# Order of projections, state products and token transfers in a fused attention and expert kernel

## The reference

```python
xn = layernorm(x)
x = x + attention(xn) + experts(xn)
# attention: 16 heads of 16 features, chunks of 64 tokens, sequences of 256
q = (q @ fq1_w.T + fq1_b) * (q @ fq2_w.T + fq2_b)      # k likewise with fk1, fk2
kv = cumsum over chunks of (kc^T vc), shifted by one chunk
o = (qc @ kv) + tril(qc @ kc^T) @ vc                   # state product + values
o = rms_norm_per_head(o) * norm_w; return o @ wo.T
# experts: 8, hidden 512; per token the most probable experts up to a sum of 0.9
probs = softmax(xn @ router_w.T); w = top_p_weights(probs, 0.9)
out += w[:, e] * ((silu(xn @ gate_w[e].T) * (xn @ up_w[e].T)) @ down_w[e].T)
```

## Time and profile before

| What | Value |
|---|---|
| median of 3 runs | 766.76 us (766.34 to 768.1) |
| profiled execution | 765.0 us |
| its span, first to last instruction | 763.3 us |
| mean granted TensorE clock | 0.973 |
| PE busy | 715.8 us (94%) |
| DVE busy | 495.6 us (65%) |
| ACT busy | 404.0 us (53%) |
| POOL busy | 346.1 us (45%) |

### The profile page before, as it was taken

How to read it: one execution, slowest core, us unless ns; L and a number is a source line. 1 busy time by engine, 2 the same in 40 slices (tenths; PEclk the granted TensorE clock), 3 DMA queues, 4 the chain that set the end, 5 groups by cost and what they waited for, 6 DMA issues and landing times.

```text
span 763.3 us, 19612 instructions
## 1 busy us (share of the span) xinstructions
PE 715.8 (94%) x6616; PEld 659.2 (86%) x6617; DVE 495.6 (65%) x1149; ACT 404.0 (53%) x923; POOL 346.1 (45%) x371
## 2 busy tenths in 40 slices
PE   8589999999999994799999999999999999999993
PEld 7467777777777773799999999999999999999992
DVE  5377887879788788365655754755754756656652
ACT  4236465555646546254655654655654655555551
POOL 3001202211120612266666766666766666666663
PEclk9799999999999998799999999999999999999997
DMA  2431211213120302543543643633643634543332
GB/s 93 131 85 48 66 56 55 59 52 111 34 77 28 76 9 70 178 101 58 110 97 58 136 70 56 145 63 57 134 72 57 144 63 79 120 63 57 63 60 31
DMA packets 51860, 59.58 MB, mean 78 GB/s; under 512 B 9344, under 2 KB 48256, under 8 KB 51840
## 3 DMA queue, kind: packets, MB, share of 16 engines
q0 software_dynamic: 19776, 27.16, 22.3%
q1 hardware_dynamic: 32064, 32.16, 14.2%
HBM read 37.15 MB, written 22.15 MB: 78 GB/s over the span
## 4 chain that ended last, share of the span: by engine, by line
PE 79%; DVE 11%; issue 4%; DMA 2%; ACT 2%; SPq 1%; POOL 0%; DVEq 0%; ACTq 0%; POOLq 0%
PE ring L1120 10%; PE ring L1121 10%; PE ring L1122 10%; PE A L1120 9%; PE A L1121 9%; PE A L1122 9%; DVE s_sb L801 4%; PE ring L1166 3%; PE S L1122 3%; PE S L1121 3%; PE S L1120 3%; PE A L1347 3%; PE ring L1188 3%; PE S L1194 2%; DMA xa<-x 1%
## 5 line engine op out<-in xcount | busy, mean ns | idle before, releaser
L473 POOL DMA_INDIRECT out<-ybuf,s_idx x98 | 161.8, 1651 | 62.6 <-POOL s_idx L469 46.6
L457 POOL DMA_INDIRECT xg<-gather_table,g_idx x100 | 100.5, 1005 | 88.2 <-issue 62.2
L1095 DVE TENSOR_TENSOR h_lo<-h,h_hi 128x256 fp32r<-128x256 f32 x196 | 83.5, 426 | 79.4 <-ACT h_hi L724 79.4
L724 ACT ACTIVATE h_hi<-h 128x256 fp32r<-128x256 f32 x196 | 82.0, 418 | 64.8 <-DVE h L1091 56.8
L1120 PE MATMUL ring<-w_hi,h_hi 128*128 128x256 f32 x392 | 113.7, 290 | 0.4 <-DVE h_lo L1095 0.4
L1120 PE MATMUL A<-gT_hi,w_hi 128*128 128x256 f32 x392 | 110.2, 281 | 1.8 <-DVE gT_lo L1064 1.8
L1121 PE MATMUL A<-gT_lo,w_hi 128*128 128x256 f32 x392 | 109.9, 280 | 0.0
L1122 PE MATMUL A<-gT_hi,w_lo 128*128 128x256 f32 x392 | 109.7, 280 | 0.0
L1122 PE MATMUL ring<-w_hi,h_lo 128*128 128x256 f32 x392 | 109.5, 279 | 0.0
L1121 PE MATMUL ring<-w_lo,h_hi 128*128 128x256 f32 x392 | 109.5, 279 | 0.0
L373 POOL TENSOR_TENSOR on_lo<-on,on_hi 128x512 fp32r<-128x512 f32 x15 | 19.3, 1288 | 143.4 <-ACT on_hi L534 143.4
(11 more groups left out here) (221 smaller groups left out, 2055.1 us busy)
## 6 DMA issues: line engine op xcount, KB each, us to landing
w_raw<-wffn SPq DMA_DIRECT2D x72, 192.0 KB
xa<-x SPq DMA_DIRECT2D x8, 512.0 KB, 4.7
gather_table<-xna SPq DMA_DIRECT2D x8, 512.0 KB, 3.1
xr<-x SPq DMA_DIRECT2D x8, 512.0 KB, 4.2
out<-yout SPq DMA_DIRECT2D x8, 512.0 KB
out<-ybuf,s_idx POOLq DMA_INDIRECT x104, 3.9
xg<-gather_table,g_idx POOLq DMA_INDIRECT x100
w_raw<-wqk_nat SPq DMA_DIRECT2D x1, 512.0 KB, 4.9
```

The lines of the kernel that those rows point to most:

```text
L457: pool.indirect_dma_start(out=xg[:, sub, :], out_offset=None, in_=table, in_offset=bass.IndirectOffsetOnAxis(ap=g_idx[:, sub:sub + 1], axi ...
L473: pool.indirect_dma_start(out=out, out_offset=bass.IndirectOffsetOnAxis(ap=s_idx[:, sub:sub + 1], axis=0), in_=ybuf[:, sub, :], in_offset= ...
L724: a.activation(h_hi[:, ic, :], h[:, ic, :], ACT.Copy).then_inc(hhi_ok, 1)
L1095: v.tensor_tensor(h_lo[:, ic, :], h[:, ic, :], h_hi[:, ic, :].bitcast(F32), ALU.subtract).then_inc(hlo_ok, 1)
```

## The change

Five things are reordered; no instruction is added or taken away.

1. SP sends the first normalised tokens to the table and loads the second 512 tokens before it waits for the split and loads the first expert's weights.
2. At the end of a round and in the set-up, the first half's queries are projected and multiplied before its keys, with the banks exchanged (queries in A3 and A0, keys in A1 and A2). ACT masks these queries at the end of the round before instead of at its start, ahead of t2k and of the second half's `head_rstd`; DVE makes queries and keys before the second half's `head_norm`. PE makes the first scores before value product 1.
3. In `values`, the two state products (now `earlier_chunk`) come before quarter 0 of a half and open its sum; the values are added to them.
4. DVE makes the first half of the one-hot before it masks the first state, in rounds 1 to 6.
5. In round 0 DVE takes the third step of the choice after masked scores 4 and 5.

```diff
--- before.py
+++ after.py
@@ -228,8 +228,8 @@
                        (S_both[:, :, :], ring[:, 1:3, :]), (S_both[:, :, :], ring[:, 1:3, :])]
         ring_first = (1, 1, 0, 1)
 
-        k_banks = [(A[3], A[0]), (A[0], A[3])]
-        q_banks = [(A[1], A[2]), (A[1], A[2])]
+        k_banks = [(A[1], A[2]), (A[0], A[3])]
+        q_banks = [(A[3], A[0]), (A[1], A[2])]
         values_banks = [A[0], A[1], A[3], A[3]]
         kt_banks = [A[0], A[1]]
         wo_banks = [A[3], A[0]]
@@ -239,7 +239,7 @@
         ms_banks = S
         xt_banks = [A[3], A[0]]
 
-        fused_order = [(3, A[0]), (2, A[3]), (1, A[2]), (0, A[1])]
+        fused_order = [(1, A[0]), (0, A[3]), (3, A[2]), (2, A[1])]
 
         names = ("small_in vo_in natural masks counts feat_ok fused_ps fused_ok split_ok setup_dve setup_act "
                  "x_in xn_ok xt_ps xhi_ok xlo_ok lg_ok proj_ps t2_ok qk_ok qz_ok xstat_ok v_ps v_ok kt_ps kt_ok kv_ps kv_ok "
@@ -277,17 +277,17 @@
             sp.dma_start(wvr_raw, wvr).then_inc(vo_in, DMA)
             sp.dma_start(wo_raw, wo).then_inc(vo_in, DMA)
 
+            def tokens_out(s):
+                sp.dma_start(table_blk[s][:, :, 0:D], xna[:, :, :]).then_inc(table_in, DMA)
+
+            sp.wait_ge(xn_ok, 1)
+            tokens_out(0)
+            sp.dma_start(xa[:, :, :], x_blk[1]).then_inc(x_in, DMA)
             sp.wait_ge(split_ok, 2)
             for piece in range(PIECES):
                 cols = slice(piece * PW, (piece + 1) * PW)
                 sp.dma_start(w_raw[:, cols], wffn[0][:, cols]).then_inc(w_in, DMA)
 
-            def tokens_out(s):
-                sp.dma_start(table_blk[s][:, :, 0:D], xna[:, :, :]).then_inc(table_in, DMA)
-
-            sp.wait_ge(xn_ok, 1)
-            tokens_out(0)
-            sp.dma_start(xa[:, :, :], x_blk[1]).then_inc(x_in, DMA)
 
             def round_of(s, first, last, more):
                 if not first:
@@ -550,7 +550,7 @@
 
             def keys2(s, half):
 
-                act.wait_ge(proj_ps, 8 * s + (1, 7)[half])
+                act.wait_ge(proj_ps, 8 * s + (3, 7)[half])
                 a.activation(t2k[:, half, :], k_banks[half][1][:, :], ACT.Identity,
                              bias=smalls[:, 4 * DK + 3:4 * DK + 4]).then_inc(t2_ok, 1)
 
@@ -567,14 +567,14 @@
 
             def queries_masked(s, half):
 
-                act.wait_ge(qk_ok, 4 * s + half + 2)
+                act.wait_ge(qk_ok, 4 * s + (1, 3)[half])
                 for par in range(2):
                     last = a.activation(qz[:, half, par, :], q[:, half, :], ACT.Copy, scale=parity[:, par:par + 1])
                 last.then_inc(qz_ok, 1)
 
             def queries2(s, half):
 
-                act.wait_ge(proj_ps, 8 * s + (3, 5)[half])
+                act.wait_ge(proj_ps, 8 * s + (1, 5)[half])
                 a.activation(t2q[:, half, :], q_banks[half][1][:, :], ACT.Identity, bias=bq2[:, 0:1],
                              scale=DK ** -0.5).then_inc(t2_ok, 1)
 
@@ -606,7 +606,6 @@
 
             def round_of(s, first, last):
 
-                queries_masked(s, 0)
                 values_out(s, 0)
                 values_out(s, 2)
                 values_out(s, 1)
@@ -639,10 +638,11 @@
                     return
                 squares(s, 1)
                 head_rstd(s, 0)
+                queries2(s + 1, 0)
+                heads_hi(s, 0)
+                queries_masked(s + 1, 0)
                 keys2(s + 1, 0)
-                heads_hi(s, 0)
                 head_rstd(s, 1)
-                queries2(s + 1, 0)
 
             token_rstd(0)
             norm_apply(0, True)
@@ -660,8 +660,9 @@
             fused_hi(3)
             act.wait_ge(setup_dve, 1)
             act.wait_ge(counts, 1)
+            queries2(0, 0)
             keys2(0, 0)
-            queries2(0, 0)
+            queries_masked(0, 0)
             round_of(0, True, False)
             with act.Fori(1, NBLK - 1) as s:
                 round_of(s, False, False)
@@ -781,15 +782,15 @@
 
             def queries(s, half):
 
-                dve.wait_ge(t2_ok, 4 * s + half + 2)
-                dve.wait_ge(proj_ps, 8 * s + (4, 6)[half])
+                dve.wait_ge(t2_ok, 4 * s + (1, 3)[half])
+                dve.wait_ge(proj_ps, 8 * s + (2, 6)[half])
                 v.scalar_tensor_tensor(q[:, half, :], q_banks[half][0][:, :], smalls[:, 4 * DK:4 * DK + 1], t2q[:, half, :],
                                        ALU.add, ALU.mult).then_inc(qk_ok, 1)
 
             def keys(s, half):
 
-                dve.wait_ge(t2_ok, 4 * s + (1, 4)[half])
-                dve.wait_ge(proj_ps, 8 * s + (2, 8)[half])
+                dve.wait_ge(t2_ok, 4 * s + (2, 4)[half])
+                dve.wait_ge(proj_ps, 8 * s + (4, 8)[half])
                 v.scalar_tensor_tensor(k[:, half, :], k_banks[half][0][:, :], smalls[:, 4 * DK + 2:4 * DK + 3],
                                        t2k[:, half, :], ALU.add, ALU.mult).then_inc(qk_ok, 1)
 
@@ -928,6 +929,8 @@
                 if not last:
                     norm_refine(s + 1, chain)
                 softmax_head(s, chain)
+                if not first and not last:
+                    one_hot(s - 1, 0)
                 state(s, 0)
                 queries(s, 1)
                 if last:
@@ -940,7 +943,8 @@
                 choose(s, 1, chain)
                 if last:
                     add_indices(s - 1)
-                choose(s, 2, chain, first)
+                if not first:
+                    choose(s, 2, chain, first)
                 if last:
                     masked_scores(s, 4)
                     slots(s, 0, chain, last_rank_bank)
@@ -952,10 +956,10 @@
                     state(s, 1)
                     masked_scores(s, 7)
                     return
-                if not first:
-                    one_hot(s - 1, 0)
                 masked_scores(s, 4)
                 masked_scores(s, 5)
+                if first:
+                    choose(s, 2, chain, first)
                 if not first:
                     one_hot(s - 1, 1)
                 masked_scores(s, 6)
@@ -968,9 +972,9 @@
                 slots(s, 0, chain)
                 slots(s, 1, chain)
                 head_norm(s, 0, chain)
+                queries(s + 1, 0)
                 keys(s + 1, 0)
                 head_norm(s, 1, chain)
-                queries(s + 1, 0)
 
             chain = Chain(dve, dve_step, None)
             norm_stats(0, chain)
@@ -1015,8 +1019,8 @@
             v.memset(keep[:, :, :], 0.0).then_inc(yr_ok, 2)
             v.memset(sm[:, :], 0.0).then_inc(idx_ok, 1)
             dve.wait_ge(counts, 1)
+            queries(0, 0)
             keys(0, 0)
-            queries(0, 0)
             round_of(0, True, False, chain)
             dve.reg_mov(chain_reg, chain.n)
             with dve.Fori(1, NBLK - 1) as s:
@@ -1168,25 +1172,30 @@
                         if n == 1:
                             last.then_inc(s_ps, 1)
 
+            def earlier_chunk(s, half):
+
+                pe.wait_ge(kv_ok, 2 * s + half + 1)
+                for b in range(2):
+                    second = slice((2 * b + 1) * P, (2 * b + 2) * P)
+                    mm(O[half][:, second], kv[:, half, b, :], q[:, half, second], start=(b == 0), stop=True,
+                       skip_group_check=True)
+
             def values(s, quad):
 
                 half, chunk = quad // 2, quad % 2
                 if quad == 0:
                     pe.wait_ge(v_ok, TT * s + TT)
-                if chunk == 1:
-
-                    pe.wait_ge(kv_ok, 2 * s + half + 1)
-                    for b in range(2):
-                        second = slice((2 * b + 1) * P, (2 * b + 2) * P)
-                        mm(O[half][:, second], kv[:, half, b, :], q[:, half, second], start=False, stop=True,
-                           skip_group_check=True)
-                pe.wait_ge(s_ok, NPAIR * s + 2 * (quad + 1) + (1 if chunk == 0 else 0))
+                if chunk == 0:
+                    pe.wait_ge(s_ok, NPAIR * s + 2 * quad + 3)
+                    earlier_chunk(s, half)
+                else:
+                    pe.wait_ge(s_ok, NPAIR * s + 2 * quad + 2)
                 for n in range(4):
                     t, par = n // 2 * 2 + chunk, n % 2
                     for g in range(PAIRS):
                         w = vz[:, t, half * PAIRS + g, 2 * par:2 * par + 2, :].rearrange("p a d -> p (a d)")
                         last = mm(O[half][32 * g:32 * g + 32, t * P:(t + 1) * P], w, s_sb[:, (PAIRS * quad + g) % NS, n, :],
-                                  start=(chunk == 0 and n == 0), stop=True, skip_group_check=True, tile_position=(0, 32 * g))
+                                  start=False, stop=True, skip_group_check=True, tile_position=(0, 32 * g))
                 last.then_inc(pv_ps, 1)
 
             def mean_squares(s, half):
@@ -1215,7 +1224,7 @@
                 o.then_inc(wo_ps, 1)
 
             def keys_by_token(s, half):
-                pe.wait_ge(qk_ok, 4 * s + (1, 4)[half])
```

(19 more changed lines are left out.)

## The result

The changed kernel takes **756.4 us** (median of 4 runs, 754.72 to 756.92), the kernel before 766.82 beside it (766.34 to 768.1): a ratio of 0.9854 [0.984, 0.9868], so 10.4 us less. The forecast was 5.3 us less: its sign and its largest term held, its size did not. The profiled execution spans 755.2 us and took 756.91.

What follows compares the result with a forecast made beforehand. PE was taken to bound a round, with DVE close behind. The sum -10.1 + 0.6 + 0.3 + 3.9 = -5.3 us took the 766.76 us median to 761.5 us; range 756.0 to 764.5, the forecast's own 758.5 to 764.5.

Steps and rivals of the forecast that it cites:

- Part 1: Set-up: second tokens loaded ahead of expert weights, first state product earlier; -10.1 us, bounds -8.2 and -10.5.
- Part 2: Round 0: choice of experts after two masked scores, PE's 2.13 us wait stays; 0 us, bounds -3.8 and +0.1.
- Part 3: State products first: PE waits for the masked state in the second half; +0.57 us in each of rounds 0 to 6.
- Part 4: Round's turn, queries before keys: late second head norm delays statistics and logits; +0.55 us per turn, bounds -0.37 and +0.8.
- Part 5: Half a one-hot moved into DVE's wait for the state product: PE's 0.34 us wait goes; -0.34 us.
- +0.78: Forecast change of a steady round, 0.55 - 0.34 + 0.57 us, paid by rounds 2 to 6.
- The first: Rival: rounds gain as edits suggest, PE's 0.71 us idleness goes in six rounds; -14.4 us, 752.4 us; chance 0.12.
- The second: Rival: new waits drop PE's clock behind the fourth value product, seven turns, 11.9 us in all; 773.4 us; chance 0.06.
- The third: Rival: set-up, second tokens still land near 28.8 us, so -10.1 falls away; 771.6 us; chance 0.04.

Runs made afterwards that it cites:

- part 1 alone: Kernel before with only the second tokens' load moved ahead of the expert weights on SP: 755.93 us, ratio 0.9841.
- the one with the shape alone changed: Changed kernel with state products back between the values, each 128*128 state product cut into four 128*32 ones: 753.26 us, ratio 0.9805.
- the last two kernels: Second head norm ahead of keys, state products at each half's end, one-hots and round 0 transposes moved; state products 128*32: 747.02 us, or 128*128: 746.48 us.
- state between: Changed kernel with the two state products of a half put back between its two quarters of values: 755.68 us, ratio 0.9838.
- head norm first: Changed kernel with the second head norm back ahead of the keys on ACT and DVE, queries still first: 751.78 us, ratio 0.979.
- part 4 undone: Changed kernel with keys projected before queries again at the turn of a round, banks as before: 757.25 us, ratio 0.9846.
- the last kernel of the experiments: The reordered version without PE's waits, its state products in 128*128 tiles instead of 128*32, still at each half's end: 746.48 us, ratio 0.9719.

## Why the prediction was half right

**Part 1** was right: -10.44 us at the first state product for a forecast of -10.1, no wait of PE from 14 to 35 us, clock 1.00; the kernel with part 1 alone carries the whole gain.

**Part 2** was right: PE waits 2.17 us at 37.16 instead of 2.13; nothing is won.

**Part 3 is the step that failed**, at the sentence "the four matmuls are the same, only the order differs", by which the first half of the round cost 0 and the second the whole wait. The wait itself was sized well (0.61 us for 0.57). But in their new place the state products follow a projection of their own tile shape instead of standing between two groups of another. The first half's passage went from 2.98 to 2.65 us, with four changes of shape and two. In the second half the stretch up to the one-hot product went from 2.73 us (185.38 to 188.11, from the first values) to 2.50 (175.13 to 177.63, from the state products, which start out of their wait); three changes lie in it before, behind one ahead of 185.38, and two now. Together that is 0.33 + 0.23 = 0.56 us a round that the sum did not have, and it takes back most of the 0.68 us by which the second half's first product comes later. The kernel with the order undone (0.10 us a round) and the one with the shape alone changed (2.65 us) show both halves of this. No idle time in the kernel before shows this, since PE counts as busy through a change; only the tiles in its rows (128\*128 and 128\*32 in the earlier trace rows) do. The Trainium skill has it, in "TensorEngine Tiling (Array Packing)", section "Key Properties": changing the tiling mode drains TensorE. The traces agree, as far as the weight load shows it, which does not run ahead into the state products across a change; whether the drain or the late load takes the time, no run separates. The page gives no time; these traces give 0.14 to 0.19 us a change in this passage.

**Part 4** was right in mechanism and close in size. DVE's statistics start at 154.27; shifted by the 10.61 us by which this round starts earlier, the forecast is 164.95 - 10.61 = 154.34. The fourth value product starts at 156.64 (forecast 156.67), behind 0.70 us of wait for the logits where "about 1" was foretold, and the projection is 0.44 us late for 0.55. Both experiments on it confirm the 0.44 and the wait, by the rounds of their traces.

**Part 5** was right: the 0.34 us wait is gone, and the way from the second half's first scores to the product that makes its state takes 6.31 us (167.60 to 173.91) instead of 6.73 (178.11 to 184.84): 0.42 less for 0.34.

A steady round is then 0.44 - 0.42 + 0.68 - 0.33 - 0.23 = +0.14, as by the starts (33.56 to 33.70), not +0.78 (0.68 is the masked state in the second half, its 0.61 us wait included). Rounds 2 to 6 so cost 0.7 us in all instead of 3.9. In round 0 the trace has -0.10 for +0.57, in round 1 -0.33 for +0.3: the same half microsecond each. In the last round -0.70 stands for 0: two changes of shape (0.33) and a wait of 0.19 us for masked scores that it had at 268.47; of the rest no row was singled out. Together -10.87 us at the last round instead of -5.3; the medians show -10.4.

**The rivals.** The first gave 752.4: its edits do not gain in the rounds as written (33.70 us), though the last two kernels show that 32.1 to 32.3 was there for another order. The second falls: the granted clock is 1.00 from 85 to 275 us, with ten waits of 0.61 and 0.70 us in it. The third falls with the statistics at 20.21.

**The range.** 756.4 us lies inside the stated 756.0 to 764.5 only because the range had been widened towards the first rival, whose mechanism did not occur; that is luck. The forecast's own range, 758.5 to 764.5, missed.

## What to carry to other kernels

Read the tile column of PE's rows as closely as its idle time: where matmuls of different tile shapes alternate, the changes cost time that shows as busy. So reordering "the same matmuls" has a price or a gain of its own, to be read from the length of a whole passage and not from its waits. Stalls of 0.1 to 0.2 us also hide there: an empty view of waits does not exclude them. And when a chain is moved forward on one engine, work out what now stands behind it in that engine's order: here queries first cost 0.44 us a turn only because the second head norm was moved back with them (round 33.26 with keys first, 33.70 as written, 32.78 with the head norm back in its place).

## What had not been expected of the hardware

A change of PE's tile shape costs 0.14 to 0.19 us between fp32 matmuls in the first half's passage: the same work takes 2.98, 2.98 and 2.99 us with four changes (before, part 1 alone, state between), 2.84 with three, and 2.65, 2.65 and 2.64 with two (the changed kernel, and two with tiled state products). Four 128\*32 tiles in place of a 128\*128 one are no slower: to the next start all sixteen take 0.55 us (127.93 to 128.48) and the four 0.54 (165.18 to 165.72), each with a change behind and none ahead. With one ahead as well the four take 0.64 (128.75 to 129.39).

A wait of PE of 2.1 to 2.2 us, at 37 to 38 us in round 0, was followed by quite different clocks over the same 9 us (36 to 45): 1.00 with part 1 alone, 0.81 in the changed kernel and the two with the state products between the values, 0.65 with the head norm first, 0.57 with part 4 undone, whose execution lost about 5 us. Behind the 1.30 us wait of the last two kernels it was 1.00. In a comparison of two profiles this stretch has to be set apart, or it is put down to the edit.

A half of the one-hot on DVE took 1.22 us at 160.14 and 2.04 at 171.37 in the changed kernel. POOL's two additions of the residual lie beside the second one (171.06 to 174.55), and the rows show that the two operations do not run together. When such a one-hot starts, 0.96 us of POOL's first addition are left here, 0.43 with the head norm first and 0.17 in the kernel before; the one-hot takes 2.04, 1.51 and 1.25 us, 1.08 more each time, in all steady rounds. POOL's second addition, which starts inside it, takes 2.08 us in the changed kernel, where 1.27 are enough in the last kernel of the experiments with no one-hot beside it. With the state products back between the values, the one-hot and the first addition start together (137.77 and 137.76): the one-hot takes 1.21 us and the addition 2.35. In the kernel with the tiles between the values 0.98 us were left and the one-hot took 2.06; it is the one that delayed the masked scores there.
